# Self attention's periods in three rounds of four score tiles, masks and whole-array work, then values

## What is computed

```python
for l in range(4):
    h = rmsnorm(x, n1[l])
    q, k, v = split(h @ Wqkv[l].T + bqkv[l])          # 16 heads of 8
    q, k = rope(q), rope(k)
    x = x + merge_heads(sdpa(q, k, v, causal_bias)) @ Wo[l].T + bo[l]
    ...                                               # cross attention to 77 tokens
    ...                                               # gated feed-forward
```

## Time and profile before

| | us |
|---|---|
| median of 3 runs | 2166.22 (2162.46 to 2178.07) |
| the profiled execution | 2163.22 |
| its span | 2161.5 |
| self attention, four stretches (layers 0 to 3) | 254, 210, 197, 202 |

### The profile page before, as it was taken

One profiled execution on the slowest core, in us unless ns is written; L12 is line 12 of the kernel. 1 busy time (PEld: TensorE's weight loads), 2 busy tenths in 40 slices (PEclk: granted clock), 3 DMA queues, 4 the chain that ended last, 5 costly groups with the idle time before them and its releaser, 6 DMA issues.

```text
span 2161.5 us, 34224 instructions
## 1 busy us (share of the span) xinstructions
PE 1847.2 (85%) x12747; PEld 1122.3 (52%) x12747; DVE 1450.1 (67%) x3531; ACT 1068.2 (49%) x1519; POOL 666.2 (31%) x903
## 2 busy tenths in 40 slices
PE   5978998594777888898989998989999998989966
PEld 4556665373544444565544564644455554456543
DVE  8667765643677777864577784567786467787468
ACT  2655665131453465564456566266656346656510
POOL 3121102503534353310455320255330245431030
PEclk9989998586796898999899999999999979999978
DMA  6342333121000000141000033000014000004100
GB/s 221 104 137 97 106 104 92 47 82 38 20 1 13 1 1 13 34 104 46 15 1 1 3 90 80 28 1 1 1 51 116 6 15 1 2 21 103 49 0 20
DMA packets 80745, 100.88 MB, mean 47 GB/s; under 512 B 31462, under 2 KB 46190, under 8 KB 79940
## 3 DMA queue, kind: packets, MB, share of 16 engines
q1 hardware_dynamic: 78532, 94.50, 15.4%
q0 software_dynamic: 2048, 4.20, 0.7%
HBM read 52.43 MB, written 12.38 MB: 30 GB/s over the span
## 4 chain that ended last, share of the span: by engine, by line
PE 41%; DVE 15%; ACT 6%; issue 4%; POOL 1%; SPq 1%; DMA 1%; DVEq 0%; POOLq 0%; ACTq 0%
PE wide L822 29%; PE acc L822 11%; DVE maxima L1747 6%; ACT prob L1989 2%; DVE hid L1251 1%; DMA masked_q<-q_g 1%; DVE x L1808 1%; ACT prob L1912 1%; DVE qkv L1715 1%; DVE moments L1294 1%; SPq L746 1%; DVE hid L1418 1%; DVE hn L1339 1%; ACT hn L1877 1%; POOL rstd L2051 1%
## 5 line engine op out<-in xcount | busy, mean ns | idle before, releaser
L1747 DVE TENSOR_REDUCE maxima<-wide 128x2 f32<-128x512 f32 (+3 forms) x512 | 406.5, 819 | 159.3 <-PE wide L822 156.7
L1989 ACT ACTIVATE prob<-wide 128x768 f32<-128x768 f32 (+1 forms) x384 | 332.6, 881 | 160.1 <-PE wide L822 159.6
L1912 ACT ACTIVATE prob<-wide 77x1024 f32<-77x1024 f32 x256 | 258.0, 1017 | 99.0 <-PE wide L822 98.9
L822 PE MATMUL wide<-q_g 32*128 32x256 f32 (+3 forms) x2048 | 274.7, 405 | 35.0 <-ACT prob L1989 16.8
L2215 POOL TENSOR_SCALAR_AFFINE_SELECT prob<-prob 128x256 f32<-128x256 f32 (+1 forms) x384 | 186.9, 491 | 352.9 <-ACT prob L1989 350.5
L1427 DVE TENSOR_REDUCE maxima<-wide 128x8 f32<-128x616 f32 x256 | 203.0, 796 | 118.6 <-PE wide L822 117.2
L822 PEld LDWEIGHTS wide<-q_g 32*128 32x128 f32 x2048 | 144.3, 196 | 212.2 <-issue 101.2
L2051 POOL TENSOR_TENSOR rstd<-moments,cst 128x4 f32<-128x4 f32 x88 | 89.8, 1020 | 522.0 <-DVE moments L1315 277.6
L1833 ACT ACTIVATE q_g<-wide 128x1024 fp32r<-128x1024 f32 x128 | 131.1, 1024 | 184.4 <-PE wide L822 184.4
L1833 ACT ACTIVATE q_g<-acc 128x512 fp32r<-128x512 f32 x192 | 114.5, 596 | 170.0 <-PE acc L822 169.6
L822 PE MATMUL wide<-kx,q_g 128*128 128x312 f32 x512 | 179.8, 417 | 7.7 <-DVE maxima L1427 4.7
(11 more groups left out here) (243 smaller groups left out, 3006.8 us busy)
## 6 DMA issues: line engine op xcount, KB each, us to landing
masked_q<-q_g SPq DMA_DIRECT2D x448, 64.0 KB
masked_q<-mask_l SPq DMA_DIRECT2D x84, 308.0 KB
masked_k<-kx SPq DMA_DIRECT2D x224, 19.5 KB, 2.3
A<-in_w SPq DMA_DIRECT2D x2, 2048.0 KB, 12.9
unit_w<-in_unit_w SPq DMA_DIRECT2D x8, 448.0 KB, 3.7
ffn_w<-in_ffn_w SPq DMA_DIRECT2D x4, 768.0 KB, 4.4
slots_in<-v_third SPq DMA_DIRECT2D x1, 2560.0 KB, 13.6
prob<-slots_in SPq DMA_DIRECT2D x8, 320.0 KB, 3.1
```

Source lines behind the costliest of these rows:

```text
L822: return e.matmul(out, lhsT, rhs, start=start, stop=stop, is_transpose=turn)
L1747: e.tensor_reduce(top[:, t, h], v[:, :, at0:at0 + P * t + P], AX.X, ALU.max, negate=True).then_inc(*made("max", *([("free", tile)] if t == ...
L1912: e.activation(p[0:SC, :], s[0:SC, :], ACT.Exp, bias=0.0, scale=1.0).then_inc(*made("exp", pb, ("free", tile)))
L1989: e.activation(pv, sv, ACT.Exp, bias=0.0, scale=8 ** -0.5).then_inc(*made("exp", pb, ("free", tile)))
```

## The change

A period gets 15 rows in place of 14, and three rounds of five. In each round PE does four tiles of 32-row products, logits, scores, logits, scores; then the causal masks of both scores tiles and all work of the whole array (transpositions, projections); then values. `causal_max` on PE is split into `causal_scores` (the products) and `causal_mask` (the mask); DVE's part, `causal_max`, stands behind the mask. `self_full` moves from row 1 to row 3, and `o_turn` with `o_norm` to row 3 of a phase of its own behind `finish`, beside `out_turn` and `out_project`. V0 moves to the next period. On PE:

```diff
--- before.py
+++ after.py
@@ -305,7 +305,9 @@
 
 
 
-SELF_ROWS = 14
+
+
+SELF_ROWS = 15
 
 
 def in_rows(*placed):
@@ -320,60 +322,65 @@
         return in_rows((6, ("stats", "s", l, b)), (8, ("variance", "s", l, b)), (12, ("apply", "s", l, b)))
 
     def project_in(b):
-        return in_rows((0, ("turn", "s", l, b)), (4, ("qkv", l, b, 0)), (8, ("qkv", l, b, 1)))
+        return in_rows((3, ("turn", "s", l, b)), (8, ("qkv", l, b, 0)), (13, ("qkv", l, b, 1)))
 
     def rotate(b, *rows):
         return in_rows(*[(row, ("rotate", l, b, k)) for k, row in rows])
 
     def prepare(b, g):
         if (l, b, g) == (0, 0, 0):
-            return in_rows((11, ("qk_turn", l, b, g)))
+            return in_rows((13, ("qk_turn", l, b, g)))
         if (l, b) == (0, 0) and g < 3:
 
             return beside(in_rows((8, ("qk_turn", l, b, g))),
                           in_rows((0, ("stats", "s", l, 1)), (2, ("variance", "s", l, 1)), (4, ("apply", "s", l, 1)),
-                                  (8, ("turn", "s", l, 1)), (10, ("qkv", l, 1, 0)), (12, ("qkv", l, 1, 1)))
+                                  (8, ("turn", "s", l, 1)), (13, ("qkv", l, 1, 0)), (13, ("qkv", l, 1, 1)))
                           if g == 1 else rotate(1, *[(k, 3 * k) for k in range(5)]))
         if b == 0 and l:
 
             return beside(in_rows((8, ("qk_turn", l, b, g))),
-                          [in_rows((4, ("turn", "s", l, 1)), (10, ("qkv", l, 1, 0))),
+                          [in_rows((8, ("turn", "s", l, 1)), (13, ("qkv", l, 1, 0))),
                            [],
-                           beside(in_rows((0, ("qkv", l, 1, 1))), rotate(1, (0, 2), (1, 4), (2, 7), (3, 10))),
-                           beside(rotate(1, (4, 0), (5, 2)), in_rows((5, ("cut_q", l, 1)), (11, ("cut_k", l, 1))))][g])
+                           beside(in_rows((3, ("qkv", l, 1, 1))), rotate(1, (0, 4), (1, 7), (2, 10), (3, 13))),
+                           beside(rotate(1, (4, 0), (5, 2)), in_rows((6, ("cut_q", l, 1)), (12, ("cut_k", l, 1))))][g])
         phase, c = in_rows((8, ("qk_turn", l, b, g))), b + 1
         if c < B:
             phase = beside(phase, *[[normalise(c)],
-                                    [project_in(c), rotate(c, (0, 10), (1, 12))],
-                                    [rotate(c, (2, 2), (3, 6), (4, 10))],
-                                    [rotate(c, (5, 0)), in_rows((4, ("cut_q", l, c)), (10, ("cut_k", l, c)))]][g])
+                                    [project_in(c), rotate(c, (0, 14))],
+                                    [rotate(c, (1, 0), (2, 4), (3, 8), (4, 12))],
+                                    [rotate(c, (5, 0)), in_rows((6, ("cut_q", l, c)), (12, ("cut_k", l, c)))]][g])
         return phase
 
-
     def scores(b, g):
-        return in_rows(*[(2 * k + 1, ("causal_max", l, b, g, k)) for k in range(len(CAUSAL_TILES))])
+        placed = []
+        for n in range(3):
+            row, pair = 5 * n, [(l, b, g, k) for k in (2 * n, 2 * n + 1)]
+            placed += [(row, ("causal_scores", *pair[0])), (row + (2 if n else 1), ("causal_scores", *pair[1]))]
+            placed += [(row + 2, (kind, *at)) for at in pair for kind in ("causal_mask", "causal_max")]
+        return in_rows(*placed)
 
     def attend(b, g):
         logits = lambda j, h0: ("self_logits", l, b, g, j, h0)
-        return in_rows((1, ("self_full", l, b, g)), (4, logits(0, 2)), (6, logits(0, 0)), (8, logits(1, 2)),
-                       (10, logits(1, 0)), (12, ("self_values", l, b, g, 0)))
+        return in_rows((3, ("self_full", l, b, g)), (6, logits(0, 0)), (9, logits(0, 2)), (11, logits(1, 0)), (14, logits(1, 2)))
 
     def finish(b, g):
         logits, values = (lambda h0: ("self_logits", l, b, g, 2, h0)), (lambda j: ("self_values", l, b, g, j))
         if (b, g) == (B - 1, G - 1):
 
-            s = [(0, logits(2)), (0, logits(0)), (1, values(1)), (2, values(2)), (2, values(3))]
+            s = [(0, logits(0)), (0, logits(2)), (1, values(0)), (2, values(1)), (2, values(2)), (2, values(3))]
             s += [(2, ("o_out", "s", l, b, 1)), (4, ("o_turn", "s", l, b, 1)), (4, ("o_norm", "s", l, b, 1))]
             return in_rows(*s, (5, ("out_turn", "s", l, b)), (7, ("out_project", "s", l, b)))
-        s = [(0, logits(2)), (2, logits(0)), (4, values(1)), (8, values(2)), (10, values(3))]
-        if g % 2:
-            s += [(11, ("o_out", "s", l, b, g // 2)), (13, ("o_turn", "s", l, b, g // 2)), (13, ("o_norm", "s", l, b, g // 2))]
-        return in_rows(*s)
+        s = [(1, logits(0)), (4, values(0)), (5, logits(2)), (9, values(1)), (14, values(2)), (14, values(3))]
+        return in_rows(*s, *([(14, ("o_out", "s", l, b, g // 2))] if g % 2 else []))
+
+    def turn_out(b, g):
+        return in_rows((3, ("o_turn", "s", l, b, g // 2)), (3, ("o_norm", "s", l, b, g // 2)))
 
     def project_out(b):
-        return in_rows((4, ("out_turn", "s", l, b)), (8, ("out_project", "s", l, b)))
-
-    items = [[prepare(b, g), scores(b, g), attend(b, g), finish(b, g)] + ([project_out(b)] if g == G - 1 and b + 1 < B else [])
+        return in_rows((8, ("out_turn", "s", l, b)), (13, ("out_project", "s", l, b)))
+
+    items = [[prepare(b, g), scores(b, g), attend(b, g), finish(b, g)]
+             + ([beside(turn_out(b, g), project_out(b) if g == G - 1 else [])] if g % 2 and (b, g) != (B - 1, G - 1) else [])
              for b in range(B) for g in range(G)]
     begin = in_rows((0, ("stats", "s", l, 0)), (0, ("variance", "s", l, 0)), (2, ("apply", "s", l, 0)), (4, ("turn", "s", l, 0)),
                     (6, ("qkv", l, 0, 0)), (8, ("qkv", l, 0, 1)), (9, ("bias_o", l)))
@@ -1102,7 +1109,7 @@
                 turn_queries(s[:, 0:S], cut_queries(("sqt", l, b)), g)
                 turn_queries(s[:, S:2 * S], k_tok, g).then_inc(*made("q_turn", tile))
 
-            def causal_max(l, b, g, k):
+            def causal_scores(l, b, g, k):
                 tile = ("smax", l, b, g, k)
                 s, qk = wide[T.slot("wide", tile)], q_g[T.slot("q_g", ("sq", l, b, g))]
                 heads_in, blocks = CAUSAL_TILES[k]
@@ -1116,6 +1123,10 @@
                         mm(s[:, at1:at1 + P * t + P], qk[r, 0, P * t:P * t + P], qk[r, 1, 0:P * t + P],
                            start=t == blocks[0], stop=False)
                     at0 += P * t + P
+
+            def causal_mask(l, b, g, k):
+                tile = ("smax", l, b, g, k)
+                s, (_, blocks) = wide[T.slot("wide", tile)], CAUSAL_TILES[k]
 
                 for c in range(2):
                     bank = s[:, S * c:S * c + S].rearrange("p (i k) -> p i k", i=NI)
@@ -1234,7 +1245,8 @@
                       q_full=q_full, max=scores_max, logits=logits, values=values, o_turn=o_turn, out_turn=out_turn,
                       out_project=out_project, f0_attn=f0_attn, f0_hidden=f0_hidden, f0_down=f0_down, f0_next=f0_next,
                       gate=gate, rank=rank, f1_turn=f1_turn, f1_hidden=f1_hidden, f1_down=f1_down, f2_matmul=f2_matmul,
-                      qkv=qkv_project, bias_o=bias_o, qk_turn=qk_turn, causal_max=causal_max, self_full=self_full,
+                      qkv=qkv_project, bias_o=bias_o, qk_turn=qk_turn, causal_scores=causal_scores,
+                      causal_mask=causal_mask, self_full=self_full,
                       self_logits=self_logits, self_values=self_values, f3_hidden=f3_hidden, f3_down=f3_down,
                       m_route=m_route, m_turn=m_turn, m_bias=m_bias, m_experts=m_experts)
             for kind, *at in ORDER:
```

## The result

The changed kernel takes 2278.79 us (median of 4 runs, 2271.63 to 2292.22), the kernel before beside it 2164.34 us. The ratio is 1.052, with a 95% interval of 1.046 to 1.059: slower by 5.2%, or 114 us.

A forecast was written before the change was run, and what follows sets the result against it. The prediction took PE, busy 85% of the span, as the bound. It summed 2163.2 us profiled, +81 for stalls less drains and +31 for the clock to 2275, with 3.0 for the median 2278 us; range 2205 to 2370.

The forecast's parts named there:

- Stalls less drains: Self attention of the seventh block: buffer waits outweigh saved changes of array shape, plain period 1.35 us longer, +81 us in all.
- the walk: The prediction's step-by-step timing of PE through the new order: plain period 11.2 us, whole sample 53.0 against 47.8.
- The clock: PE's clock falls behind each sample's second QKV projection: 12 stays of 10 us at 0.26 us each, +31 us.
- DVE's chain: Second projection waits for both maxima and fill, then add, ACT's copies, next exp: 0.75 us more for the fourth tile.
- Fourth tile behind an exp: In every block the fourth tile takes the first one's buffer after ACT's exp, 1.40, 1.40 and 1.62 us from block start.
- three such waits of one: The one PE wait of 0.86 us for an exp buffer becomes three in each period, making the new order slower.
- Signs named: Plain period 11 to 11.4 us, three exp waits near 1 us, maxima releasing third tiles, clock 0.50 behind second projections.
- (1): Rival: only the stalls in self attention, clock stays as it is, 2247 us; chance 0.32.
- (3): Rival: faster, about 2091 us, as the drains at shape changes go and the fourth tile doesn't wait; chance 0.04.
- (2): Rival: clock stays down in about half of all periods, 2347 us, or 2447 if in all; chance 0.12.
- (4): Rival: no difference, PE's existing waits move into the blocks and swallow the saving, plain period 9.5 to 10.2 us; chance 0.05.

## Why the prediction was right

**The sum.** 2278 forecast, 2279 measured. That the two agree to 1 us is luck: the two terms behind the sum were off by some ten us each, in opposite directions, and most of the low clock didn't stand where the prediction put it.

- *Stalls less drains, +81 us.* About 70 to 75 by my estimate: the 114 us less what the low clock takes. At full clock the sample of 56.66 us would be 56.66 - 10.2 x 0.38 = 52.8 us; the walk said 53.0. A plain period from masks to masks is 11.00 us, the walk said 11.2. Its legs from masks to masks are 3.55, 4.34 and 3.11; the walk had 3.57, 4.34 and 3.31. The last was too long since the pair of maxima takes 2.36 us when it isn't held up (1563.52 above), not 2.56.
- *The clock, +31 us.* The extra low time was forecast as 120 us and came to 114. Its price was mis-sized: 0.35 to 0.40 us in place of 0.26, so the term is 40 to 45 us. The place was mostly wrong, and the amount right by luck. The prediction counted 12 stays of 10 us, one behind the second projection of each sample. In windows of 1 us, layers 1 to 3 have six such gaps in their 14 periods, not nine, the clock falls behind four of them, and these stays hold about 20 us. Some 47 us stand in the first two periods of the layers; the kernel before has its 55 us there and in the third. The other 65 us are 17 stays that begin 1 to 4 us ahead of the copy of `self_full` in a period with `o_turn`; for these the walk had no clock term.
- *DVE's chain.* The step with the third round's maxima, the fill, the add and the copies of V came out as told. The prediction spread the loss over all rounds and named the exp's buffer first. The runs give the weights: joined masks in the last round alone cost 83 of the 111 us that the joins cost together, and with short maxima this cost is gone.
- *Fourth tile behind an exp.* It is in the trace, 1.34 us after the block's start where 1.40 was told. But joining the masks doesn't make it: with masks on their own it stands there too, and the time is that of the kernel before. The step "three such waits of one" told the length of a plain period well and was wrong as the reason for the loss. With masks on their own the 14 periods of layers 1 to 3 take 501.6 us in all, against 499.8 before: plain periods are longer (10.40 and 11 us without and with `o_turn`, against 9.87), and less time at the low clock and shorter periods with projections (12.2 us, against 12.9, for the one with `out_project`) give it back.
- *Signs named.* PE's weight loads wait 139.1 us for exp against 43.1; DVE's maxima release the third tile; rows at 0.50 stand behind four of the six second projections. Two signs failed. The plain period between two copies of `self_full` is 12.02 us at a mean clock of 0.91, not 11 to 11.4; only masks to masks at full clock is it 11.00. And a plain period has two waits for an exp ahead of a fourth tile, not three, of 0.54 and 0.27 us in the bracket, not near 1 us; in the third block PE waits for DVE instead. The bracket counts only from the modelled end of the last product, so it reads lower than the distance of starts.

**The rivals.** (1), stalls without the clock, 2247: excluded by the low time, and below the fastest run of 2271.63. (3), faster, fell, and the Trainium skill's rule that a change of tiling mode drains the engine (TensorEngine Tiling (Array Packing), Key Properties) didn't decide: even with readers cut short the order with fewer changes is 40 us behind. (2) fell: low time was 259 of some 980 us in self attention, not half. (4) fell with plain periods of 11.0 us; the waits did move into the blocks, but they took more than was saved.

## What to carry to other kernels

Whoever groups work of one shape keeps the tiles of the group in their buffers until the group is through, and so delays every reader of the first tile. Price that with the longest reader on the far engine and with what is queued behind it there; a saved round trip of 0.33 us is small beside two reductions of 1.2 us that start late. Put work that needs none of the contended buffers (here the values) between the tiles, not behind them; here it was worth 1.2%. Look at the periods with extra work too, not only at the plain one: there the queue of the reading engine is longest. And read where the clock falls instead of placing it at the longest gap.

## What was not expected

- The clock doesn't fall behind the same gap each time: behind two of six equal gaps it stayed at 1.00, and with the short exp a sample ran at a mean of 0.84 in layer 1 and the same one at 1.00 in layer 3. Where it falls, the gap costs twice, as stall and as low clock.
- Repeated 32-row products did not hold the clock: low time went from 135 to 199 us.
- Waits in the list that grow aren't proof of a cause. With the short maxima the wait for exp grew from 139.1 to 172.7 us while the kernel became some 105 us faster.

Still open is why the joins of neighbouring rounds don't add up, if they don't: the evidence is barely clear of noise, and the extra time stands in the first four periods of a layer, which no run took apart. Open too is why the clock falls behind one gap and not behind its equal.
